# Head sums by token tile, and two VectorE jobs given to GpSimd, in a cross-attention pair on one core

## What is computed

```python
q = split(rmsnorm(x, gamma_q) @ Wq.T)                 # 16 heads of 16
k, v = split(kn @ Wk.T), split(kn @ Wv.T)             # kn = rmsnorm(ctx, gamma_kv)
mask = abs(ctx_pos - idx[:, :, None]) <= 1
w = where(mask, square(relu(q @ k.T / sqrt(hd))), 0)
denom = maximum(w.sum(-1, keepdims=True), EPS_DEN)
x = x + ((w / denom) @ v) @ Wo.T
# second block
q, k, v = gelu(x @ Wq1 + bq), gelu(ctx @ Wk1 + bk), gelu(ctx @ Wv1 + bv)
x = softmax(q @ k.T) @ v @ Wf + bf + x
out = (x - mean) * rsqrt(var + 1e-05) * ln_gamma + ln_beta
```

## Time and profile before

| what | number |
|---|---|
| median of 3 runs | 348.92 us (348.28 to 348.96) |
| the profiled execution | 349.19 us, of it span 347.4 us |
| PE busy | 332.7 us (96%) |
| DVE busy | 307.8 us (89%) |
| ACT busy | 242.2 us (70%) |
| POOL busy | 169.7 us (49%) |
| mean granted PE clock | 0.988 |
| HBM read, written | 16.77 MB, 8.39 MB |

### The profile page before, as it was taken

One profiled execution on the slowest core, in us unless ns is written; L12 is line 12 of the kernel. 1 busy time (PEld: TensorE's weight loads), 2 busy tenths in 40 slices (PEclk: granted clock), 3 DMA queues, 4 the chain that ended last, 5 costly groups with the idle time before them and its releaser, 6 DMA issues.

```text
span 347.4 us, 5599 instructions
## 1 busy us (share of the span) xinstructions
PE 332.7 (96%) x1930; PEld 240.7 (69%) x1930; DVE 307.8 (89%) x486; ACT 242.2 (70%) x486; POOL 169.7 (49%) x203
## 2 busy tenths in 40 slices
PE   7999999999999999999999999999999999999980
PEld 3575778868686767676868677776767686857750
DVE  1689598999999999999999989999999999999766
ACT  4599433486868695959595959596877868685752
POOL 4315020025656473839283747474747566444424
PEclk9899999999999999999999999999999999999997
DMA  7975615903232222323141414141414132010103
GB/s 238 315 219 149 199 57 131 248 17 129 83 117 94 102 98 79 109 66 126 63 149 60 152 61 151 62 150 62 150 63 144 67 133 80 2 60 2 60 0 122
DMA packets 21819, 37.96 MB, mean 109 GB/s; under 512 B 2144, under 2 KB 8288, under 8 KB 21792
## 3 DMA queue, kind: packets, MB, share of 16 engines
q1 hardware_dynamic: 18816, 29.48, 27.2%
q0 software_dynamic: 2016, 7.34, 6.1%
q10 hardware_dynamic: 960, 0.79, 0.7%
HBM read 16.77 MB, written 8.39 MB: 72 GB/s over the span
## 4 chain that ended last, share of the span: by engine, by line
PE 79%; DVE 13%; ACT 3%; DMA 2%; issue 1%; ACTq 0%; DVEq 0%
PE ps L498 12%; PE ps L499 12%; PE ps L500 12%; PE ps L577 7%; PE ps L549 7%; PE ps L543 6%; PE ps L635 4%; PE ps L670 4%; PE ps L752 4%; PE ps L743 4%; DMA vfd<-wv0T 2%; PE ps L530 2%; PE ps L640 2%; DVE qkp L1259 2%; DVE kv L1221 2%
## 5 line engine op out<-in xcount | busy, mean ns | idle before, releaser
L1259 DVE TENSOR_TENSOR qkp<-ps,bufs 128x1024 f32<-128x1024 f32 x48 | 55.7, 1215 | 0.9 <-PE ps L543 0.8
L377 POOL TENSOR_TENSOR x_lo<-x_ring,x_hi 128x1024 fp32r<-128x1024 f32 x16 | 38.0, 2373 | 37.7 <-ACT x_hi L998 37.7
L418 POOL TENSOR_TENSOR bufs<-bufs,lng_twice 128x1024 f32<-128x1024 f32 x14 | 33.8, 2411 | 28.3 <-ACT bufs L1038 26.2
L1076 ACT ACTIVATE xp_hi<-bufs 128x512 fp32r<-128x512 f32 x28 | 17.7, 632 | 41.1 <-DVE bufs L1347 41.1
L391 POOL TENSOR_TENSOR mean_gap<-stats 128x4 f32<-128x4 f32 x14 | 2.8, 198 | 72.0 <-DVE stats L1336 65.2
L1270 DVE TENSOR_TENSOR ps<-ps,wn 128x1024 f32<-128x1024 f32 x31 | 37.9, 1224 | 0.0
L420 POOL TENSOR_TENSOR bufs<-bufs,lnb_row 128x1024 f32<-128x1024 f32 x14 | 33.3, 2378 | 1.1
L577 PE MATMUL ps<-qkp,cst 128*32 128x512 f32 x192 | 30.7, 598 | 0.0
L577 PE MATMUL ps<-bufs,cst 128*32 128x512 f32 x64 | 30.5, 598 | 0.0
L1002 ACT ACTIVATE bufs<-ps 128x512 f32<-128x512 f32 x32 | 19.2, 603 | 16.1 <-PE ps L500 16.0
L498 PE MATMUL ps<-x_hi,wh_q 128*128 128x512 f32 x64 | 26.6, 415 | 0.0
(11 more groups left out here) (257 smaller groups left out, 933.3 us busy)
## 6 DMA issues: line engine op xcount, KB each, us to landing
x_ring<-xT SPq DMA_DIRECT2D x16, 512.0 KB, 3.5
out<-bufs POOLq DMA_DIRECT2D x14, 512.0 KB, 3.4
idx_ring<-idx SPq DMA_DIRECT2D x16, 256.0 KB, 3.9
wkv_lo<-kv SPq DMA_DIRECT2D x32, 126.0 KB
kvs<-kv SPq DMA_DIRECT2D x30, 126.0 KB
vfd<-bufs SPq DMA_DIRECT2D x8, 256.0 KB, 4.5
qkp<-ctxT SPq DMA_DIRECT2D x2, 512.0 KB, 6.8
kv<-kv_cross SPq DMA_DIRECT2D x8, 128.0 KB, 4.1
```

What stands on the lines that cost most here:

```text
L377: G.tensor_tensor(x_lo[:, :, :], x_ring[:, e % RING, :, :], f32_view(x_hi[:, :, :]), ALU.subtract).then_inc(xl_ready, 2)
L418: G.tensor_tensor(zo, zn, lng_twice[:, :].unsqueeze(1).broadcast_to([P, TT, D]), ALU.mult).then_inc(zg_ready, 1)
L1259: V.tensor_tensor(qk[:, s, :, :], ps[:, bank0:bank0 + 2, :], q0, ALU.mult).then_inc(qk_ready, 1)
```

## The change

Four things change.

1. `head_sums` stands by token tile. Each of the four narrow matmuls takes one tile of 128 tokens and all three shifts, so it moves 3x128 = 384 columns, where it moved 512. The squares of `x` no longer go through PE: rows of `x` (tokens on partitions) are loaded by a DMA of their own, 512 KB a batch, and ACT squares and sums them in four instructions of 256 columns with the accumulator. DVE takes the floor from SBUF in one `scalar_tensor_tensor`. The ReLU moves 384 columns, and three transposes stand where four stood.
2. The sum of UP and DOWN, on DVE before (L1356), is made by POOL (`pair_sum`), with both products in SBUF. It stands between the gamma scaling and `x_lo`; the beta scaling moves behind `x_lo`. In the tail DVE still adds for the last batch.
3. The one-hot of batches 1 to 15 is built on POOL, at the head of POOL's step.
4. The rows of `x` for batch 0 are loaded behind the context rows, those of batch 1 between `cross(3)` and `cross(4)`, the others at the end of SP's step.

The diff, cut to its core:

```diff
 def head_sums(a):
     pe.wait_ge(qk_ready, 3 * a + 3)
-    pe.wait_ge(xsq_ready, a + 1)
     for g in range(DC):
-        for s in range(SHIFTS + 1):
-            i = mm(ps[32 * s:32 * s + 32, 0, :], sum_sel[:, g if s < SHIFTS else 2, :],
-                   qk[:, s, g, :] if s < SHIFTS else xsq[:, g, :], start=(g == 0), stop=(g == DC - 1))
+        for j in range(TT):
+            i = mm(ps[32 * j:32 * j + 32, 0, 0:SHIFTS * P].rearrange("p (s t) -> p s t", s=SHIFTS), sum_sel[:, g, :],
+                   qk[:, :, g, j * P:(j + 1) * P], start=(g == 0), stop=(g == DC - 1))
...
 # ACT
 def square_x(a):
-    if a > 0:
-        act.wait_ge(s_mm, a)
-    A(xsq, x_ring[:, a % RING, :, :], ACT.Square).then_inc(xsq_ready, 1)
+    act.wait_ge(rows_in, 16 * a + 16)
+    if a > 1:
+        act.wait_ge(dcl_ready, a - 1)
+    for j in range(TT):
+        A(x_rows[:, j, :], x_rows[:, j, :], ACT.Square, scale=FLOOR_SCALE,
+          accum_out=floor[:, a % 2, j:j + 1]).then_inc(floor_ready, 1)
...
-A(s_sb[:, :], ps[:, 0, :], ACT.Relu, bias=den_eps).then_inc(s_cp, 1)
+A(s_sb[:, 0:SHIFTS * P], by_shift, ACT.Relu).then_inc(s_cp, 1)
...
 # PE, the transposes of the weights, and the wait ahead of the DOWN keys
-    for j in range(TT):
+    for s in range(SHIFTS):
...
-    pe.wait_ge(sum_ready, 2 * f + 1)
+    pe.wait_ge(att_ready, 3 * f + 2)
     picked_keys(a, DOWN, 0)
...
 # SP
+def load_rows(i):
+    if i > 0:
+        sp.wait_ge(floor_ready, TT * i)
+    sp.dma_start(x_rows, x[i].rearrange("(j p) d -> p j d", p=P)).then_inc(rows_in, 16)
...
 # POOL
+def build_onehot(a):
+    pool.wait_ge(idx_in, 16 * a + 16)
+    pool.wait_ge(cst_in, 16)
+    if a > 1:
+        pool.wait_ge(vg_mm, 3 * (a - 1))
+    G.tensor_scalar(onehot[:, a % 2, :], idx_ring[:, a % RING, :], pos, None, ALU.is_equal).then_inc(onehot_ready, 1)
+def pair_sum(f):
+    pool.wait_ge(att_ready, 3 * f + 2)
+    G.tensor_tensor(att[:, 1, :, :], att[:, 0, :, :], att[:, 1, :, :], ALU.add).then_inc(pair_ready, 1)
...
 def step(e, a, f, b, n):
+    if a is not None and f is not None:
+        build_onehot(a)
     if n is not None:
         norm_factors(n)
-        scale_rows(n)
+        scale_gamma(n)
+    if f is not None:
+        pair_sum(f)
     if e is not None and e > 1:
         split_x_lo(e)
     if n is not None:
+        scale_beta(n)
         write_rows(n)
...
 # DVE
     dve.wait_ge(att_ready, 3 * b + 3)
-    dve.wait_ge(sum_ready, 2 * b + 1)
+    dve.wait_ge(pair_ready, b + 1)
     V.tensor_tensor(att_flat(0), picked(2), att_flat(1), ALU.add).then_inc(sum_ready, 1)
...
-if a is not None and f is not None:
-    build_onehot(a)
...
-V.tensor_tensor(dcl[:, :, :], den[:, :, :], den_floor.broadcast_to([P, TT, H]), ALU.max).then_inc(dcl_ready, 1)
+dve.wait_ge(floor_ready, TT * f + TT)
+V.scalar_tensor_tensor(dcl[:, :, :], floor[:, f % 2, :].unsqueeze(2).broadcast_to([P, TT, H]), 16.0 * EPS_DEN * EPS_RMS,
+                       den[:, :, :], ALU.add, ALU.max).then_inc(dcl_ready, 1)
...
-attend(f, 1, DOWN, 0, picked(0))
-dve.wait_ge(att_ready, 3 * f + 2)
 if b is not None:
-    dve.wait_ge(sum_ready, 2 * b + 2)
-V.tensor_tensor(att_flat(1), picked(0), att_flat(0), ALU.add).then_inc(sum_ready, 1)
+    dve.wait_ge(sum_ready, b + 1)
+attend(f, 1, DOWN, 0, att_flat(1))
```

More of the change, by code:

```diff
@@ L15, with xattn_pair @@
 LN_EPS = 1e-05
+FLOOR_SCALE = (16.0 * EPS_DEN / D) ** 0.5
 CT = B * K // P
 RING = 3
-C_ID, C_SEL, C_POS, C_EPS, C_END = 0, 128, 224, 225, 226
+C_ID, C_SEL, C_POS, C_END = 0, 128, 192, 193
 CENTRE, UP, DOWN = range(SHIFTS)
-def xattn_pair(nc: bass.Bass, xT, ctx, ctxT, idx, vectors, wq0T, wk0T, wv0T, wo0T,
+def xattn_pair(nc: bass.Bass, xT, x, ctx, ctxT, idx, vectors, wq0T, wk0T, wv0T, wo0T,
                wq1, wk1, wv1, wf1, bf1, ln_g, ln_b, consts, out):
@@ L99, in xattn_pair @@
         bufs = sb("bufs", [P, 8, DC * T])
-        xsq, q0, xpT, q1T = (bufs[:, n, :].rearrange("p (c t) -> p c t", c=DC) for n in (0, 3, 4, 5))
+        q0, xpT, q1T = (bufs[:, n, :].rearrange("p (c t) -> p c t", c=DC) for n in (3, 4, 5))
+        x_rows = bufs[:, 0, :].rearrange("p (j d) -> p j d", j=TT)
+        floor = sb("floor", [P, 2, TT])
         zn, zo = (bufs[:, n, :].rearrange("p (j d) -> p j d", j=TT) for n in (6, 7))
@@ L134, in xattn_pair @@
             "vec_in", "cst_in", "wk1_in", "wkv_in", "wq0_in", "wv1_in", "wf1_in", "w1_in", "ln_in", "x_in", "idx_in"))
+        rows_in = sem("rows_in")
         ctxT_in = [sem("ctxT_in0"), sem("ctxT_in1")]
@@ L158, in xattn_pair @@
         twice_ready = sem("twice_ready")
+        pair_ready, last_pair = sem("pair_ready"), sem("last_pair")
         kvs_zero = [sem(f"kvs_zero_{r}") for r in range(2)]
@@ L295, in _ @@
             context_rows()
+            load_rows(0)
             weight(raw["v1"], wv1, wv1_in)
@@ L314, in _ @@
             cross(3)
+            load_rows(1)
             cross(4)
@@ L338, in step @@
                     shifted(e)
+                if e is not None and e >= 2:
+                    load_rows(e)
             steps(step)
@@ L462, in _ @@
             norm_factors(OLD - 1)
-            scale_rows(OLD - 1)
+            scale_gamma(OLD - 1)
+            scale_beta(OLD - 1)
             write_rows(OLD - 1)
@@ L630, in step @@
                 if b is not None:
-                    pe.wait_ge(sum_ready, 2 * b + 2)
+                    pe.wait_ge(sum_ready, b + 1)
                     for g in range(DC):
@@ L765, in old_turn @@
             def old_turn():
-                pe.wait_ge(sum_ready, 2 * OLD + 2)
+                pe.wait_ge(sum_ready, OLD + 1)
                 for g in range(DC):
@@ L773, in last_weights @@
                 pe.wait_ge(s_cp, LAST + 1)
-                for j in range(TT):
-                    i = nc.tensor.transpose(ps[:, 0, j * P:(j + 1) * P], s_sb[:, j * P:(j + 1) * P], ident)
+                for s in range(SHIFTS):
+                    i = nc.tensor.transpose(ps[:, 0, s * P:(s + 1) * P], s_sb[:, s * P:(s + 1) * P], ident)
                 i.then_inc(sT_mm, 1)
@@ L1113, in last_sums @@
                 act.wait_ge(s_mm, LAST + 1)
-                A(s_sb[:, :], ps[:, 0, :], ACT.Relu, bias=den_eps).then_inc(s_cp, 1)
+                A(s_sb[:, 0:SHIFTS * P], by_shift, ACT.Relu).then_inc(s_cp, 1)
             def last_squares():
                 act.wait_ge(sT_mm, LAST + 1)
-                by_row = w.rearrange("p s j h -> p j s h")
+                by_row = w.rearrange("p s j h -> p (s j) h")
                 A(by_row, by_row, ACT.Square).then_inc(w_ready, 1)
@@ L1399, in last_weights @@
                 dve.wait_ge(den_ready, LAST + 1)
-                V.tensor_tensor(dcl[:, :, :], den[:, :, :], den_floor.broadcast_to([P, TT, H]), ALU.max).then_inc(dcl_ready, 1)
+                dve.wait_ge(floor_ready, TT * LAST + TT)
+                V.scalar_tensor_tensor(dcl[:, :, :], floor[:, LAST % 2, :].unsqueeze(2).broadcast_to([P, TT, H]), 16.0 * EPS_DEN * EPS_RMS,
+                                       den[:, :, :], ALU.add, ALU.max).then_inc(dcl_ready, 1)
                 dve.wait_ge(dcl_ready, LAST + 1)
@@ L1413, in last_second @@
                 dve.wait_ge(att_ready, 3 * LAST + 2)
-                dve.wait_ge(sum_ready, 2 * OLD + 2)
-                V.tensor_tensor(att_flat(1), picked(0), att_flat(0), ALU.add).then_inc(sum_ready, 1)
+                dve.wait_ge(sum_ready, OLD + 1)
+                V.tensor_tensor(att_flat(1), picked(0), att_flat(0), ALU.add).then_inc(last_pair, 1)
             def half_third(h):
```

27 lines of the change are left out of this document (11 added, 16 removed).

## The result

The changed kernel takes 343.73 us (median of 4 runs, 343.50 to 344.14), the one before 348.60 us beside it on the same chip. The ratio is 0.9863, with a 95% interval of 0.9844 to 0.9882: 4.87 us faster, where 2.5 us were forecast. The profiled execution has a span of 342.0 us, where the one before had 347.4 us.

What follows compares the result with a forecast made beforehand. PE was taken as the bound, tied with DVE at the transposes of the summed products. Terms -3.9 - 0.55 + 1.7 + 0.25 = -2.5 took the profiled 349.19 to 346.7, as a median 346.4 us; range 344.0 to 349.5.

Steps and rivals of the forecast that it cites:

- Term 1: Transposes of the summed products, where PE and DVE are tied: 0.28 us saved in each of 14 steps, 3.9 less.
- term 3: Start: later ACT, POOL and DVE work and POOL's one-hot delay `v_hi` and `v_lo`, and PE shows it: 1.7 us more.
- the start costs nothing, or PE gets more: Rival, chance 0.17: one-hot passes `v_hi` or DVE holds on, 344.4; or PE's whole 0.44 arrives, term 1 becomes 7.7.
- Term 2: Batch 1, without `nmax` between, gives its full 0.55 us less; batch 0 gives nothing, as PE waits for `v_lo`.
- Term 4: First pair sum on POOL meets DVE's splits of `o0` and `q1`; PE's L549 waits: 0.25 us more.
- ACT's squares: ACT in a full step: 1.7 us, perhaps 2.2 with accumulator reads, for 1.05; hidden in 2.71 us of idle time.
- the row loads: Last in SP's step, a whole step ahead of the squares, 512 KB a batch: costed at nothing.
- POOL's queue: One-hot of 1.4 us ends before the next layernorm, cover 0.6; rival that it becomes the bound, chance 0.11: 350.3 to 355.
- `dcl`: In a full step beside a DMA issue, costed at nothing; rival that it falls behind the one-hot, chance 0.14: 368.

Runs made afterwards that it cites:

- before_again: The kernel before, unchanged, profiled once more: 348.44 us.
- sums_only: The changed kernel with pair sum and one-hots back on DVE and the beta scaling where it stood before: 345.16 us, ratio 0.9911 to the kernel before.
- moves_only: The kernel before with only the pair sum and the one-hots moved to POOL; head sums, squares and floor as before: 347.86 us, ratio 1.0.
- after_again: The changed kernel, unchanged, run once more: 343.02 us, ratio 0.9847 to the kernel before.
- onehot1_dve: The changed kernel with the one-hot of batch 1 built by DVE: 342.66 us, ratio 0.9838 to the kernel before.
- sums_half: The changed kernel with half of the head sums left out: 343.97 us, ratio 0.988 to the kernel before.
- scores_early: `onehot1_dve` with PE's two score transposes moved ahead of the last two of the eight transposes of `xpT`: 339.88 us, ratio 0.9766 to the kernel before.
- the two halves: `sums_only` and `moves_only`, each half of the change alone against the kernel before: 345.16 and 347.86 us.
- pair kernels: Three kernels without the reference's computation, running one POOL and one DVE instruction on own tiles at varied offsets; a DVE instruction lost 0.27 us beside the one-hot.
- start_dve: The changed kernel with the one-hot of batch 1 and the pair sum of batch 0 back on DVE: 342.80 us, ratio 0.9843 to the kernel before.

## Why the prediction was wrong

The direction and the steady part held; the start was put about 2 us too dear. For the start, the traces with the clock at 1.00 give two stretches of PE: from its first head sum to its first use of `v_hi`, and from there to the first layernorm.

| run | to `v_hi` | to the layernorm |
|---|---|---|
| `before_again` | 7.22 | 42.76 |
| `sums_only` | 6.72 | 42.23 |
| `moves_only` | 7.23 | 43.06 |
| `after_again` | 7.08 | 42.36 |
| `onehot1_dve` | 6.71 | 42.38 |

- **Term 1**, "14 x 0.28 = 3.9 us less": right. From the first layernorm to the end it measured 268.54 - 264.34 = 4.2. The chain was the one described: the transposes start 2.03 behind the score transposes. `sums_half` shows that nothing of PE's further saving arrives, `scores_early` that the chain set the pace, and the two halves that PE and DVE had been tied.
- The step that failed is **term 3**, "1.7 more", with "So each waits for the other's whole instruction" beneath it. It measured 0.36 in the time and 7.08 - 6.71 = 0.37 in the first stretch (`onehot1_dve` against the changed kernel), 1.3 less than put. A one-hot on POOL holds `v_lo` for 0.37 only. I had drawn the rule from `v_hi`, which ended 0.28 behind the clearing, but that was a copy in the last part of the clearing, and `v_lo` is a subtraction in the first part of the one-hot. The Trainium skill ("SBUF — State Buffer", "SBUF: two separate sides") says that the lock is held for the whole instruction. By the pair kernels a `tensor_scalar` on POOL doesn't hold DVE for its whole length (0.55 of 1.56 us); there the measurement decides. A `tensor_tensor` on POOL held everything that came up to 0.82 behind its start until its end; nothing was tried later. The 0.4 that term 3 took for a later start of DVE and POOL isn't there either: the clearing ends 5.66 behind the first head sum in `sums_only` (33.15 - 27.49) and 5.62 in `before_again` (33.82 - 28.20). My rival "the start costs nothing, or PE gets more" comes nearest in its number (344.4), by luck: neither of its ways came about, for the one-hot came behind the start of `v_hi` and got in ahead of `v_lo`.
- **Term 2**, 0.55 for batch 1 and "Batch 0 gives nothing": half right. Between `before_again` and `sums_only` the second stretch, which has batch 1 in it, is 0.53 shorter, but so is the first by 0.50: batch 0 gives its share as well. That PE waits for `v_lo` there was true of the execution that I read, in which the clearing and `v_lo` came over 1 us later than in `before_again`, behind the stretch of low clock; in `before_again` PE doesn't wait. A single trace was taken for the usual case.
- **Term 4**, "0.25 more": right in the trace. The order was as expected (copy, pair sum, subtraction, copy, subtraction), the pair sum held `wl_o` to its end, and PE lost 0.28 at the place named. In the medians it can't be told apart.
- Sum of the misses: for the two stretches 1.4 more was forecast, and 0.14 + 0.40 = 0.5 less was measured, a miss of 1.9. Of it 1.3 is term 3 and 0.5 batch 0. Term 1 adds 0.3. Together this is 2.2, where 2.4 were missing (4.9 less 2.5); the rest is within what the first 28 us differ from one execution to another.
- ACT's squares, the row loads, POOL's queue and `dcl` cost nothing in a full step, as forecast: DVE's products now wait for ACT's copy of `q0` (8.0 us in 13 waits), but that copy itself waits for PE, and no wait for the row loads shows. The one-hot is 1.60 us for 1.4, and the cover at the next layernorm 0.39 for 0.6.

## What to carry to other kernels

Where two engines reach one place at the same moment, relieving either gives only part (0.5 and 1.7 us of the steady time here, 0.1 and 2.8 in all), and both together give more than the sum (4.2, and 4.9 in all). Once the gain stops at a wait, read what that wait's own chain waits for: two transposes put 0.2 us earlier in each step were worth 2.8 us, and nothing before the change. And a cost read from one row of the start holds for that pair of instructions at that offset only; the start of a second execution should be read before it is used.

## What the runs showed of the hardware that I had not expected

A `tensor_scalar` on POOL shuts DVE out of SBUF in two parts. For the clearing (2.77 us) these are the first 0.9 us, against the subtraction, the copy and the small `scalar_tensor_tensor` alike, and its last third against the copy and not against the subtraction (the small instruction wasn't tried there). A copy that came at 1.60 got through and one at 1.80 didn't; in the whole kernels `v_hi` got through at 1.69 (`start_dve`) and not at 1.75 (the kernel before, 33.99 - 32.24). For the one-hot (1.56 us) they are the first 0.55 us, and the end for a copy that came at 1.00 or later (one at 0.80 got through). A copy that gets in just ahead of the last part makes POOL longer instead (1.68 for 1.56, 2.91 for 2.77, and 3.00 for 2.77 in `start_dve`). A `tensor_tensor` on POOL (1,024: 2.34 us) held every DVE instruction that came up to 0.82 behind its start until its end: the copies all ended 0.28 behind it, the subtractions 0.54 to 0.55. Later ones weren't tried.

The granted clock fell to 0.50 between 11 and 15 us in 2 of 12 traces. The second of these, of `start_dve`, is of a run at 343.4 us, where the fastest of that kernel took 342.48.
